# One more tile of layer-norm statistics ahead of the normalisation, in a fused attention and mixture layer on eight cores

## The chip, the cores and the metric

The kernel runs on the 8 cores of one Trainium2 chip. Cores 0 to 3 are one die, cores 4 to 7 the other. No core talks to another. The metric is device time in microseconds of the slowest core; a lower time is better.

## The reference

Input x is (4, 2048, 2048) float32. It is layer-normalised over its last axis, and the layer adds two branches to it:

```python
xn = layernorm(x)                        # no scale, no bias, eps 1e-5
q, k, v = xn @ Wq.T, xn @ Wk.T, xn @ Wv.T        # 16 heads of 128
attn = softmax(q k^T / sqrt(128)) v      # per head, over 2048 tokens
base = xn @ W_base.T + b_base
e = argmax(softmax(xn @ router_W.T))     # one of 8 experts
delta = ((xn @ A.T) * onehot(e)) @ Bw * 2.0      # rank 16 per expert
x = x + attn @ Wo.T + base + delta
```

## The kernel before

**Who does what.** Core c takes sequence c//2 and owns 1024 of its 2048 tokens. It computes keys and values for all 2048 tokens, and queries and outputs for its own. The host lays the tokens out so that a core's own come first (`xtok`).

**Stages.** First the layer-norm stage: 16 tiles of 128 tokens, each 128 x 2048 float32, 1 MB, are loaded, normalised to bf16, transposed on TensorE and left in `xnT` for good. Then `gen_proj` makes queries, keys and values of head 0, and for each head h attention of head h-1 is woven with the projections of head h. At the end come the output projection and the mixture branch (`gen_dpre`, `dpost`). Every matmul of a projection reads all of `xnT` (`XNALL`), so the first of them (L399) can start only when the last tile of the layer-norm stage is in `xnT`.

**The layer-norm stage.** Two functions write out its order by hand, each for one tile `tc`:

- `ln_stats(tc)` (L262 on): SyncE issues the load of the tile (L267) into one of four slots, `tc % 4`: slots 0 and 1 are the halves of `xst`, slots 2 and 3 lie in `pt`. VectorE runs four bn_stats of 512 columns (L271) and one bn_aggr (L275). ScalarE then makes 1/sqrt(var + eps) with Ln and Exp (L277, L280). `st2` and `rcol` have a place of their own for each tile.
- `ln_norm(tc)` (L284 on): VectorE writes (x - mean) * rstd as bf16 into one of two `xns` buffers (L290, one instruction of 2048 columns). TensorE transposes it in 16 pieces into two PSUM banks (L298), ScalarE copies the two banks into `xnT` (L302). Behind that stand the router's 16 small matmuls for tile `tc - 1` if that is below 8 (L329, copy L334), and, from `tc` 8 on, `mask_chain(tc - 8)`: two small VectorE instructions (L315, L317), a TensorE transpose (L320) and a ScalarE copy (L323).

**What sets the order.** Each engine runs its instructions in the order in which the program emits them. `Prog.emit` adds semaphore waits from the named reads and writes. A load of tile t writes the slot that tile t-4 had, so it waits in SyncE's queue until L290 of tile t-4, the last reader, is done. SyncE has only loads and stores to do, so it can run far ahead of the other engines otherwise. The emission loop is

```python
ln_stats(0)
ln_stats(1)
for tc in range(NTC):
    ln_norm(tc)
    ln_stats(tc + 2)
```

and gives VectorE the order S0 S1 N0 S2 N1 S3 N2 ... S15 N14 N15, where S is the statistics of a tile and N its normalisation (with the mask instructions behind N8 to N15). `ln_stats` returns at once for a tile past the last.

**The other loads.** GpSimd's queue issues, before any of this, the casting loads (float32 in HBM to bf16 in SBUF) of `ats`, `wbls` and head 0's `wqs`, `wks` and `wvs`, 1 MB of float32 each (L246 to L252, L378 to L386). They share the DMA engines with the tiles.

Of the kernel before, what the change touches and what calls it, by code (L numbers as in the profile page):

```python
# [147 lines left out]
def build_program(debug=False):  # L148
# [27 lines left out]
    with ExitStack() as st:  # L176
# [85 lines left out]
        def ln_stats(tc):  # L262
            if tc >= NTC:
                return
            sl = tc % 2
            xv, xk, ptk = xslots[tc % 4]
            p.emit("sync", lambda E, tc=tc, xv=xv: E.dma_start(  # L267
                xv, xtok[tc * 128:(tc + 1) * 128, :]), writes=[xk])
            s6 = st6[:, sl * 24:(sl + 1) * 24]
            for i in range(4):  # L270
                p.emit("dve", lambda E, xv=xv, i=i, s6=s6: E.bn_stats(  # L271
                    s6[:, i * 6:(i + 1) * 6], xv[:, i * 512:(i + 1) * 512]),
                    reads=[xk], writes=[f"st6{sl}"])
            s2 = st2[:, tc * 2:(tc + 1) * 2]
            p.emit("dve", lambda E, s6=s6, s2=s2: E.bn_aggr(s2, s6),  # L275
                   reads=[f"st6{sl}"], writes=[f"st2_{tc}"])
            p.emit("act", lambda E, s2=s2, sl=sl: E.activation(  # L277
                sqv[:, sl:sl + 1], s2[:, 1:2], AF.Ln, bias=epsc[:, 0:1],
                scale=1.0), reads=[f"st2_{tc}", "epsc"], writes=[f"sqv{sl}"])
            p.emit("act", lambda E, sl=sl, tc=tc: E.activation(  # L280
                rcol[:, tc:tc + 1], sqv[:, sl:sl + 1], AF.Exp, scale=-0.5),
                reads=[f"sqv{sl}"], writes=[f"rcol{tc}"])

        def ln_norm(tc):  # L284
            sl = tc % 2
            nxv, xk, ptk = xslots[tc % 4]
            xnv = xns[:, sl * D:(sl + 1) * D]
            xnk = f"xns{sl}"
            s2 = st2[:, tc * 2:(tc + 1) * 2]
            p.emit("dve", lambda E, nxv=nxv, xnv=xnv, s2=s2, tc=tc: E.tensor_scalar(  # L290
                xnv, nxv, s2[:, 0:1], rcol[:, tc:tc + 1],
                ALU.subtract, ALU.mult),
                reads=[xk, f"st2_{tc}", f"rcol{tc}"] + ptk, writes=[xnk])
            b0, b1 = (0, 1) if tc % 2 == 0 else (2, 3)
            for half, b in ((0, b0), (1, b1)):
                for j in range(8):
                    dc = half * 8 + j
                    p.emit("pe", lambda E, b=b, j=j, dc=dc, xnv=xnv: E.transpose(  # L298
                        psabf(b)[:, j * 128:(j + 1) * 128],
                        xnv[:, dc * 128:(dc + 1) * 128], idbf[:]),  # L300
                        reads=[xnk, "idbf"], writes=[f"psA{b}"])
                p.emit("act", lambda E, b=b, half=half, tc=tc: E.copy(  # L302
                    xnT3[:, half * 8:(half + 1) * 8, tc * 128:(tc + 1) * 128],
                    psabf(b).rearrange("p (a b) -> p a b", b=128)),
                    reads=[f"psA{b}"], writes=[f"xnT{tc}"])
            rtc = tc - 1
            if 0 <= rtc < 8:
                router(rtc)
            if tc >= 8:
                mask_chain(tc - 8)  # L310
# [26 lines left out]

        ln_stats(0)
        ln_stats(1)
        for tc in range(NTC):  # L340
            ln_norm(tc)
            ln_stats(tc + 2)

        def b2():
            for nb in range(2):
# [263 lines left out]
def _get_nc(debug=False):  # L609
    if debug not in _NC_CACHE:  # L610
        _NC_CACHE[debug] = build_program(debug)
    return _NC_CACHE[debug]
# [52 lines left out]
```

How the kernel before makes its waits and increments, by code:

```python
            def body(E, items=items, eng=eng):  # L133
                for it in items:
                    if it[0] == "w":
                        E.wait_ge(sem[it[1]], waitval(it[1], it[2]))
                    else:
                        instr = it[1](E)
                        sname = it[2]
                        if (sname, it[3]) in tgt:
                            instr.then_inc(
                                sem[sname],
                                16 if sname in self.dma_sems else 1)
```

## Time and profile before

| | us |
|---|---|
| median of 2 runs | 1332.82 (1332.25 to 1333.39) |
| the profiled execution, its time | 1330.53 |
| its span, slowest core (core 4) | 1329.0 |
| spans of the eight cores | 1323.3 to 1329.0 |
| first matmul of the first projection, core 4 | 98.97 |

The page and the answers below are of core 4 unless a line says otherwise. Times on a timeline count from the core's first instruction. PE is TensorE's matmuls, PEld its weight loads, DVE VectorE, ACT ScalarE, SPq SyncE's queue; "issue" is time in which an engine waited for nothing that the profile shows. On a timeline row the first number is the start, the second the duration (from the first start to the last end where instructions are merged), and the bracket is the engine's idle time before it with what ended it.

### The profile page before, as it was taken

The page shows a single profiled execution, that of the slowest core. Times are in us where ns is not written, and L with a number is a line of the kernel's source. Part 1 is how long each engine was busy: PE and PEld are TensorE (multiplying, and loading weights), DVE is VectorE, ACT ScalarE, POOL GpSimd, SP SyncE. Part 2 cuts the span into 40 slices and gives each one's busy share as a digit, 9 for nine tenths or more (in the row PEclk, how much of TensorE's full clock was granted, in tenths as well). Part 3 has the DMA queues.
Part 4 walks back from the last instruction along what each step waited for, and adds up shares of the span by engine and source line. Part 5 has one row for each costly group of instructions (what it writes and reads, how often), then busy time and mean ns, then how long its engine had stood idle before and what let it go on. Part 6 is the DMA issues. An engine that isn't in the chain of part 4 may idle for free.

```text
span 1329.0 us, 15178 instructions; the slowest of 8 cores (1323.3 to 1329.0 us)
## 1 busy us (share of the span) xinstructions
PE 1199.1 (90%) x5763; PEld 537.5 (40%) x5866; DVE 225.0 (17%) x326; ACT 403.1 (30%) x723; POOL 45.2 (3%) x89
## 2 busy tenths in 40 slices
PE   1449899999999999999999999999999997999998
PEld 1433444444443444444444434444444433444443
DVE  5871111111111111111111111111111100001001
ACT  2450233333343434333343433343333450000000
POOL 1000000000000000000000000000000000000000
PEclk9999999999999999999999999999999998999999
DMA  9831101112011111011010111110110304565774
GB/s 234 259 127 32 32 17 32 28 20 33 16 32 32 19 30 32 16 33 32 16 33 17 32 32 26 22 32 16 33 32 16 48 1 95 110 159 131 152 160 112
DMA packets 19255, 77.61 MB, mean 58 GB/s; under 512 B 2544, under 2 KB 2544, under 8 KB 17136
## 3 DMA queue, kind: packets, MB, share of 16 engines
q0 software_dynamic: 12128, 43.06, 20.2%
q1 hardware_dynamic: 7056, 33.57, 7.2%
q8 instruction: 49, 0.80, 0.2%
q14 instruction: 22, 0.18, 0.0%
HBM read 111.29 MB, written 8.39 MB: 90 GB/s over the span
## 4 chain that ended last, share of the span: by engine, by line
PE 85%; DVE 8%; DMA 4%; issue 3%; ACT 0%; DVEq 0%; SPq 0%; POOL 0%; ACTq 0%; POOLq 0%
PE psB L399 28%; PE psA L399 12%; PE psA L441 9%; PE psE L458 9%; PE psC L470 8%; PE psB L512 4%; PE psB L535 4%; PE psA L512 4%; PE psA L535 4%; DMA pt<-xtok 3%; DVE st L271 2%; DVE vt L409 2%; DVE kt L409 2%; DVE xns L290 1%; DMA wks<-wb 1%
## 5 line engine op out<-in xcount | busy, mean ns | idle before, releaser
L447 ACT ACTIVATE pt<-psA 128x512 bf16<-128x512 f32 x512 | 271.9, 600 | 353.8 <-PE psA L441 353.4
L399 PE MATMUL psB<-xnT,wvs 128*128 128x512 bf16 x751 | 216.1, 379 | 9.6 <-DVE kt L409 8.2
L399 PE MATMUL psA<-xnT,wks 128*128 128x512 bf16 x511 | 193.6, 379 | 9.0 <-DVE kt L409 8.2
L399 PE MATMUL psB<-xnT,wks 128*128 128x512 bf16 x496 | 185.3, 379 | 8.3 <-DVE qt L409 8.2
L441 PE MATMUL psA<-qt,kt 128*128 128x512 bf16 x510 | 143.0, 380 | 3.6 <-ACT vh L432 2.0
L399 PE MATMUL psB<-xnT,wqs 128*128 128x512 bf16 x497 | 118.7, 383 | 2.8 <-ACT maskT L323 2.0
L399 PEld LDWEIGHTS psB<-xnT,wvs 128*128 128x128 bf16 x768 | 74.0, 98 | 106.5 <-issue 21.6
L458 PE MATMUL psE<-pt,onesc 128*1 128x512 bf16 x512 | 115.7, 379 | 0.0
L470 PE MATMUL psC<-pt,vh 128*128 128x512 bf16 x482 | 109.4, 379 | 2.5 <-issue 2.5
L399 PE MATMUL psA<-xnT,wvs 128*128 128x512 bf16 x255 | 96.6, 379 | 0.1
L298 PE MATMUL psA<-idbf,xns 128*128 128x128 bf16 x256 | 29.9, 309 | 62.3 <-DVE xns L290 42.3
L480 DVE TENSOR_TENSOR ctall<-psC,bc 128x512 bf16<-128x512 f32 x32 | 22.1, 692 | 358.5 <-PE psA L441 311.8
L399 PEld LDWEIGHTS psB<-xnT,wks 128*128 128x128 bf16 x512 | 50.0, 98 | 72.3 <-issue 15.6
L399 PEld LDWEIGHTS psA<-xnT,wks 128*128 128x128 bf16 x512 | 50.0, 98 | 72.3 <-issue 15.6
L399 PEld LDWEIGHTS psB<-xnT,wqs 128*128 128x128 bf16 x512 | 50.5, 99 | 63.2 <-issue 4.2
L470 PEld LDWEIGHTS psC<-pt,vh 128*128 128x128 bf16 x512 | 47.5, 98 | 66.9 <-issue 14.0
L441 PEld LDWEIGHTS psA<-qt,kt 128*128 128x128 bf16 x512 | 47.5, 98 | 65.2 <-issue 13.9
L458 PEld LDWEIGHTS psE<-pt,onesc 128*1 128x1 bf16 x512 | 40.3, 83 | 67.5 <-issue 6.8
L512 PE MATMUL psB<-xnT,wks 128*128 128x512 bf16 x250 | 58.5, 387 | 6.1 <-DMA wks<-wb 5.7
L463 ACT ACTIVATE lnl<-psE 1x512 f32<-1x512 f32 x32 | 18.8, 586 | 136.7 <-PE psE L458 136.7
L535 PE MATMUL psB<-ctall,wqs 128*128 128x512 bf16 x252 | 58.0, 387 | 2.0 <-DVE ctall L480 1.8
L512 PE MATMUL psA<-xnT,vt 128*128 128x512 bf16 x251 | 57.1, 379 | 0.3
(68 smaller groups left out, 662.3 us busy)
## 6 DMA issues: line engine op xcount, KB each, us to landing
xst<-xtok SPq DMA_DIRECT2D x8, 1024.0 KB, 7.4
pt<-xtok SPq DMA_DIRECT2D x8, 1024.0 KB, 8.8
wqs<-wq POOLq DMA_DIRECT2D x16, 512.0 KB, 5.0
wks<-wk POOLq DMA_DIRECT2D x16, 512.0 KB, 5.2
wvs<-wv POOLq DMA_DIRECT2D x16, 512.0 KB, 5.0
xst<-xT SPq DMA_DIRECT2D x16, 512.0 KB, 12.0
outT<-outb SPq DMA_DIRECT2D x16, 512.0 KB, 11.1
wqs<-wo POOLq DMA_DIRECT2D x8, 512.0 KB, 8.3
```

What stands on the lines that cost most here:

```text
L271: p.emit("dve", lambda E, xv=xv, i=i, s6=s6: E.bn_stats(s6[:, i * 6:(i + 1) * 6], xv[:, i * 512:(i + 1) * 512]), reads=[xk], writes=[f"st6 ...
L298: p.emit("pe", lambda E, b=b, j=j, dc=dc, xnv=xnv: E.transpose(psabf(b)[:, j * 128:(j + 1) * 128], xnv[:, dc * 128:(dc + 1) * 128], idbf[: ...
L399: col=col, ws=ws: E.matmul(ps_t[:, col:col + 512], ws[:, dc * 128:(dc + 1) * 128], xnt(dc, nb * 512, (nb + 1) * 512), start=(dc == 0), sto ...
L409: dst=dst: E.tensor_copy(dst[:, nb * 512:(nb + 1) * 512], ps_t[:, col:col + 512]),
L441: p.emit("pe", lambda E, kc=kc, qb=qb, bk=bk, ktv=ktv, qtv=qtv: E.matmul(psa(bk), ktv[:, kc * 128:(kc + 1) * 128], qtv[:, qb * 512:(qb + 1 ...
L447: p.emit("act", lambda E, kc=kc, bk=bk: E.activation(pt[:, kc * 512:(kc + 1) * 512], psa(bk), AF.Exp, scale=SCALE), reads=[f"psA{bk}"], wr ...
L458: p.emit("pe", lambda E, kc=kc: E.matmul(psE[0:1, :], onesc[:], pt[:, kc * 512:(kc + 1) * 512], start=(kc == 0), stop=(kc == NTC - 1)), re ...
L463: p.emit("act", lambda E: E.activation(lnl[:], psE[0:1, :], AF.Ln), reads=["psE"], writes=["lnl"])
L470: p.emit("pe", lambda E, kc=kc, vhv=vhv: E.matmul(psC[:], vhv[:, kc * 128:(kc + 1) * 128], pt[:, kc * 512:(kc + 1) * 512], start=(kc == 0) ...
L480: p.emit("dve", lambda E, h=h, qb=qb: E.tensor_tensor(ctall[:, h * QOWN + qb * 512: h * QOWN + (qb + 1) * 512], psC[:], bc[:], ALU.mult), ...
L512: wbv=wbv, wbk_keys=wbk_keys, pk=pk: E.matmul(ps_t[:, off + nb * 512: off + (nb + 1) * 512], wbv[:, dc * 128:(dc + 1) * 128], xnt(dc, nb * ...
L535: p.emit("pe", lambda E, dc=dc, nb=nb, ps_t=ps_t, off=off, wot=wot: E.matmul(ps_t[:, off + nb * 512: off + (nb + 1) * 512], wot[:, dc * 12 ...
```

## The change

The loop gets one more call ahead of it, and its call inside runs three tiles ahead in place of two.

```diff
         ln_stats(0)
         ln_stats(1)
+        ln_stats(2)
         for tc in range(NTC):
             ln_norm(tc)
-            ln_stats(tc + 2)
+            ln_stats(tc + 3)
```

The buffers stay as they are: four slots for loaded tiles, two for normalised ones. No instruction is added or taken away. VectorE's order becomes S0 S1 S2 N0 S3 N1 S4 ... S15 N13 N14 N15; ScalarE's Ln and Exp of tile t stand behind the copies of tile t-3 in place of t-2. The order of the loads in SyncE's queue and what each waits for (L290 of tile t-4) are the same.

## Rows read from the trace of the kernel before

**Rows 1.** The page: header, busy time of the engines, 40 slices

```profile
span 1329.0 us, 15178 instructions; the slowest of 8 cores (1323.3 to 1329.0 us)
PE 1199.1 (90%) x5763; PEld 537.5 (40%) x5866; DVE 225.0 (17%) x326; ACT 403.1 (30%) x723; POOL 45.2 (3%) x89
PE   1449899999999999999999999999999997999998
DVE  5871111111111111111111111111111100001001
```

**Rows 2.** Timeline of TensorE, first round of the first projection; core 4, then core 7

```profile
98.97 8.47 PE L399 MATMUL psB<-xnT,wqs 128*128 128x512 bf16 x31 [2.02 <-ACT maskT L323]
...
99.72 7.07 PE L399 MATMUL psB<-xnT,wqs 128*128 128x512 bf16 x32 [1.64 <-ACT maskT L323]
```

**Rows 3.** Cores: span and mean granted TensorE clock

```profile
core 4: 1329.0 us, clock 0.996
...
core 7: 1328.3 us, clock 0.996
```

**Rows 4.** Waits of VectorE up to 98 us, longest first

```profile
DVE st L271 <- DMA xst<-xtok: 10.6, 4, 6.8
DVE st L271 <- DMA pt<-xtok: 4.8, 3, 1.8
```

**Rows 5.** Timeline of core 4, 18 to 44 us: statistics, normalisation, issues

```profile
18.48 3.08 DVE L271 BATCH_NORM_STATS2 st<-pt 128x6 f32<-128x512 f32 x4 [1.40 <-DMA pt<-xtok]
...
24.90 3.08 DVE L271 BATCH_NORM_STATS2 st<-pt 128x6 f32<-128x512 f32 x4 [1.78 <-DMA pt<-xtok]
...
28.27 1.34 DVE L290 TENSOR_SCALAR xns<-pt,st,rcol 128x2048 bf16<-128x2048 f32 x1
...
29.68 6.98 SPq L267 DMA_DIRECT2D pt<-xtok  x2
...
31.55 3.08 DVE L271 BATCH_NORM_STATS2 st<-xst 128x6 f32<-128x512 f32 x4 [1.94 <-DMA xst<-xtok]
...
43.68 3.09 DVE L271 BATCH_NORM_STATS2 st<-pt 128x6 f32<-128x512 f32 x4 [1.62 <-DMA pt<-xtok]
```

**Rows 6.** The same, 48 to 58 us

```profile
51.67 1.34 DVE L290 TENSOR_SCALAR xns<-pt,st,rcol 128x2048 bf16<-128x2048 f32 x1
...
52.92 3.08 DVE L271 BATCH_NORM_STATS2 st<-xst 128x6 f32<-128x512 f32 x4
53.08 4.95 SPq L267 DMA_DIRECT2D pt<-xtok  x2
...
57.54 3.08 DVE L271 BATCH_NORM_STATS2 st<-xst 128x6 f32<-128x512 f32 x4
```

**Rows 7.** DMA queues, 20 to 40 us: packets, MB, share of 16 engines

```profile
q0 software_dynamic: 458, 1.68, 52.0%
q1 hardware_dynamic: 458, 3.36, 51.0%
```

**Rows 8.** The same, from 71 us to the first projection

```profile
71.00 1.28 DVE L290 TENSOR_SCALAR xns<-pt,st,rcol 128x2048 bf16<-128x2048 f32 x1
72.66 3.08 DVE L271 BATCH_NORM_STATS2 st<-xst 128x6 f32<-128x512 f32 x4
...
88.08 3.08 DVE L271 BATCH_NORM_STATS2 st<-pt 128x6 f32<-128x512 f32 x4
91.44 1.28 DVE L290 TENSOR_SCALAR xns<-pt,st,rcol 128x2048 bf16<-128x2048 f32 x1
93.11 1.34 DVE L290 TENSOR_SCALAR xns<-pt,st,rcol 128x2048 bf16<-128x2048 f32 x1
93.97 2.17 ACT L302 COPY xnT<-psA 128x1024 bf16<-128x1024 bf16 x2 [1.76 <-PE psA L298]
96.19 2.15 ACT L302 COPY xnT<-psA 128x1024 bf16<-128x1024 bf16 x2
```

**Rows 9.** Loads issued from 48 to 83 us, median us to landing; core 4, then core 7

```profile
xst<-xtok SPq DMA_DIRECT2D x3, 1024.0 KB, 4.9
pt<-xtok SPq DMA_DIRECT2D x4, 1024.0 KB, 5.1
...
pt<-xtok SPq DMA_DIRECT2D x4, 1024.0 KB, 6.3
xst<-xtok SPq DMA_DIRECT2D x3, 1024.0 KB, 6.1
```

**Rows 10.** SyncE's timeline, the same tile's load on core 6, then core 7

```profile
53.62 0.33 SPq L267 DMA_DIRECT2D pt<-xtok  x1
...
54.21 0.33 SPq L267 DMA_DIRECT2D pt<-xtok  x1
```

## The prediction

> **What bounds the kernel now.** Read the page's busy shares and its 40 slices first [rows 1]. TensorE is busy 90% of the span, and from the fourth slice on (each is 33.2 us) it is full: there the time is set by matmuls, which this change does not touch. The first three slices are another stage: TensorE at 1, 4 and 4 tenths, VectorE at 5, 8 and 7. This is the layer-norm stage, and the first projection matmul, at 98.97 us on core 4 [rows 2], waits for its last copy. What moves that start moves the end by the same amount, since nothing behind it waits for a clock of its own. So the whole question is when L399 starts on each core. The spans of the cores [rows 3] say which core counts.
>
> Inside the stage, the waits of VectorE come next [rows 4]: it waited for seven loads, 15.4 us in all, of which 6.8 us is the first tile. The timeline tells two regimes apart. Up to 44 us VectorE idles 1.1 to 1.9 us before the statistics of each tile, until its load has landed [rows 5]. The tiles come every 6.3 us there (24.90 to 43.68 is three tiles). From 48 us on no load is waited for, and VectorE runs one tile in 4.62 us (52.92 to 57.54) [rows 6]; with the mask instructions, from tile 8 on, in 5.02. The first regime is bound by supply: the two DMA queues take 52% and 51% of the engines' time [rows 7], GpSimd's casting loads one half and the tiles the other. The second is bound by VectorE alone.
>
> **The change part by part.** No instruction is removed or added; VectorE's 96 large ones in this stage cost the same. Three things move.
>
> *First, the statistics wait less for their scale.* N(t) needs `rcol` from ScalarE. Before, one S stands between S(t) and N(t); after, two. But L290 shows no idle time before it [rows 5, 6, 8], only 0.18 us behind the aggregation, so nothing is won: zero.
>
> *Second, loads are issued one VectorE step later against their need.* A load of tile t is issued when N(t-4) is done. Before, VectorE had S(t-2), N(t-3), S(t-1) and N(t-2) to do from there to S(t), two periods; after, S(t-1) and N(t-3), one period. Four rows give the steps: statistics start to normalisation start 3.37 us (24.90 to 28.27), normalisation start to issue 1.4 (28.27 to 29.68), normalisation start to the next statistics 1.25 (51.67 to 52.92), or 1.66 with the mask instructions (71.00 to 72.66) [rows 5, 6, 8]. From issue to need that leaves 3.37 + 1.25 + 1.25 - 1.4 = 4.5 us in the plain tiles and 5.3 in those whose two normalisations carry masks. Before it was 4.6 to 5.0 us more, and landings of 4.9 to 6.3 us [rows 9] were hidden. Now they are not: of two tiles, one full chain is issue, landing, statistics, normalisation, so that two tiles cost L + 4.8 us and one costs (L + 4.8)/2, if that is over 4.62 (or 5.02). With core 4's landing, 4.9, this is 4.85; with core 7's, about 6.1, it is 5.45.
>
> I walked this through tile by tile for core 4. S2 starts at 18.48 and S3 at 24.90 as before, both set by landings. N0 moves behind S2, to 21.85, so tile 4 is issued at 23.2, where it was issued six microseconds earlier. It still queues behind tile 3, so that S4 comes at about 31.7 (31.55 before). How long before the landing of the tile ahead must a load be issued so that the queue does not run dry? The tiles' queue moved 3.36 MB, 3.2 tiles, in 51% of 20 us, which is 3.2 us of the engines for a tile [rows 7]; a tile that has them alone lands in 4.9 [rows 9]; the difference, 1.7 us, is what each load needs beside them (an estimate). Tiles 4, 5 and 6 are issued at 23.2, 29.7 and 36.6, and the tile ahead lands at 24.9, 31.7 and 37.9: 1.7, 2.0 and 1.3 us ahead, just enough or a little short. I allow 0.2 to 0.5 us for each: S5 at 37.9, S6 at about 44.7 against 43.68, or +1.0. (The empty time goes to the casting loads, which so end earlier.) Then S7 49.3, S8 54.4 (landing), S9 59.0, S10 63.9, S11 69.9 (the load of this tile took 6.1 us on core 4 before), S12 75.0, S13 80.4, S14 85.4, S15 90.65, against 88.08 [rows 8]. That is +2.6 us at S15. The bounds of this term: 0 if every landing shortens to what the gap hides, +2.6 with core 4's landings, +6.0 if I walk core 7 with its own (S15 at 95.25 against 89.21, with S6 0.7 late).
>
> *Third, the tail.* Behind S15 there were N14 and N15; now there are N13, N14 and N15. VectorE does a normalisation with its masks in 1.67 us (91.44 to 93.11), but ScalarE copies a tile in 2.22 (93.97 to 96.19) [rows 8], so the third tile costs ScalarE's time, not VectorE's. L399 started 7.53 us after N14 (98.97 - 91.44). Now it starts 7.53 + 2.21 = 9.74 us after N13, which is 3.37 after S15. From S15 to L399 it was 10.89 and becomes 13.1: +2.2 us. Were VectorE never late, S15 would come 1.67 earlier, having one normalisation less before it, and the tail would net +0.5; but S15 is held by loads from tile 3 on, so the whole 2.2 stands. Bounds +0.5 and +2.2; I take 2.2.
>
> The sum on core 4 is 2.6 + 2.2 = +4.8. On a core like 7 it is up to 6.0 + 2.2 = +8.2, and with L11's own slow landing and rounding in the walk, 8.7. I don't take the full value. Cores 0, 2, 5 and 7 show the long landings and 1, 3, 4 and 6 the short ones, and the long ones belong to the core of each pair that issues later: of cores 6 and 7 it is core 7, by 0.6 us [rows 10]. A core that falls behind its neighbour overlaps less with it, and its landing should approach 4.9. I take the middle between 4.8 and 8.7, +6.7.
>
> The Trainium skill, page "HBM Reference", section "Specifications (TRN2)", says that the two cores of a pair share one stack and get about 358 GB/s each when both stream. The page "DMA: Bandwidth & Descriptors" puts a fixed 2.0 us on each transfer. An estimate from the two is 1.05 MB/358 GB/s + 2.0 = 4.9 us for both cores. Core 4's row agrees, core 7's 6.1 to 6.3 does not; by the rule every core would lose 4.8.
>
> Which core ends last: core 4, 1329.0 + 4.8 = 1333.8; core 7, 1328.3 + 6.7 = 1335.0 [rows 3]. The slowest grows by 6.0 us, so the profiled execution's 1330.53 (1.5 us around its span) would become 1336.5. The median of the runs shown is 2.3 us above that execution, and the forecast against it is 1332.8 + 6.0 = 1338.8 us.
>
> **The rivals.**
>
> *The landings stay hidden or nearly so (chance 0.2).* Were the landings nowhere over 4.5 us, only the early 1.0 and the tail's 2.2 remain, +3.2; with an equal share in each pair and a clock gain (below) of 1.6 on core 4 it is 3.2 too. That gives 1333 to 1336. For it: the loads are later and farther apart, and casting loads end earlier. Against it: the medians behind 48 us are 4.9 and 5.1 even on core 4 [rows 9], and there the engines had little else to do.
>
> *Faster (chance 0.05).* One mechanism: TensorE's clock at the start of the projection. On core 4 the first round takes 8.4 us, on core 7 7.0 [rows 2]; 32 matmuls of 512 columns take 13.7 us at 1.2 GHz and 6.8 at 2.4, so core 4 began at the lower level and core 7 at the higher. Ahead of it both transposed two tiles close together. The granted clock in the records is 0.996 on both [rows 3] and doesn't tell them apart. With three tiles close together core 4 may enter at 2.4 GHz: -1.5 us on the slowest cores. It decides only if the loads cost nothing and the tail nets +0.5: 1332.8 - 1.0 = 1331.8. The first seven tiles' supply speaks against that.
>
> *Every late core pays in full (chance 0.2).* If the neighbour's traffic keeps landings at 6 us or over whatever the offset, core 7 loses 8.7: 1328.3 + 8.7 = 1337.0, +8.0, 1340.8. Should overlapping loads stretch to 7 us, the worst row among the late cores, each of the twelve tiles from 4 on costs (7 + 4.8)/2 - 5.0 = 0.9 more than before: 10.8 + 2.2 = 13, and 1345.
>
> *No change in what the program does (under 0.01):* the order of VectorE's queue must change, as emission order is queue order.
>
> **How the numbers follow.** My forecast, +4.8 to +8 us on the slowest core (1337 to 1341), has 0.55. Hidden landings have 0.2, the faster case 0.05, the full price 0.2. The time is that of the first, 1338.8. The range reaches down to the hidden case, 1333, and up to the stretched loads, 1345; about 0.1 stays out on each side. Two percent, which is about what a measurement of this kernel can tell from no change, is 26.7 us. No case comes near it, even the sum of the worst terms, 13: faster by over 2% 0.01, within 2% 0.98, slower by over 2% 0.01.
>
> **What would show it.** In the changed kernel VectorE's timeline must show waits for loads before the statistics of tiles 8 to 11 where there were none, and total waits for `xtok` of over 17 us on core 4 and over 20 on core 7. N0 starts near 21.9 us, the load of tile 4 is issued near 23.2, S15 starts near 90.7 on core 4, three normalisations stand 1.7 us apart behind it, and ScalarE's copies behind them 2.2 us apart; L399 starts near 103.8 on core 4 and near 106.4 on core 7. The prediction is wrong if landings fall under 4.5 us, if the supply in the first 45 us moves by more than 1 us per tile, or if what follows L399 is no longer the same length on each core.

## The result and the profile after

The changed kernel takes 1341.25 us (median) against 1333.25 us for the kernel before in the same comparisons. The ratio is 1.0058 with a 95% interval of 1.0045 to 1.0071: slower by 7.7 us or 0.6%, which is inside 2%. The forecast was 1338.8 us, the range 1333 to 1345. Some executions show one die disturbed; the ratios leave them out.

The answers of the profile of the changed kernel that correspond to [rows 3] (cores) come first, then VectorE's waits for loads on core 4, which [rows 4] show for before. A row of waits gives the total us, the count and the longest.

```profile
core 0: 1337.4 us, clock 0.995
...
core 4: 1329.3 us, clock 0.999
...
core 7: 1333.9 us, clock 0.995
```

```profile
DVE st L271 <- DMA xst<-xtok: 14.8, 5, 7.0
DVE st L271 <- DMA pt<-xtok: 6.5, 4, 2.3
```

The slowest core is now core 0. Core 4, the slowest before, hardly moved in this execution: 1329.3 against 1329.0. Spans alone would mislead here. The place to look is the start of the first projection round (the line is L400 now), on all eight cores:

| core | 0 | 1 | 2 | 3 | 4 | 5 | 6 | 7 | mean |
|---|---|---|---|---|---|---|---|---|---|
| start before, us | 99.92 | 98.81 | 99.52 | 98.75 | 98.97 | 99.27 | 99.14 | 99.72 | 99.3 |
| start after, us | 107.78 | 105.42 | 104.92 | 106.62 | 105.61 | 108.38 | 107.11 | 105.12 | 106.4 |
| later by | 7.9 | 6.6 | 5.4 | 7.9 | 6.6 | 9.1 | 8.0 | 5.4 | 7.1 |

So nearly the whole loss, 7.1 us on the mean, was made before that start, as the prediction said it must be; the spans are 7.4 us longer on the mean. What follows the first round takes the same time as before (1220.1 us against 1220.4, mean of the cores). The first round itself (32 matmuls, counted up to the first matmul of the next round) became 0.6 us longer on the mean, 8.0 against 7.5. Where part of it runs at TensorE's lower clock level (a matmul of 512 columns every 0.43 us and not every 0.22) it takes 8.1 to 8.7 us and not 6.7 to 6.9: before so on three cores, now on six. And the rest varies by core from 1217.0 us (core 4, granted clock 0.999) to 1222.7 (core 6, 0.996). Core 4 lost 6.6 us at the start, won 1.6 in the first round and 4.7 behind it.

Where in the stage did the loss arise? Below is VectorE's timeline on core 0 from 14 to 52 us, and from 95 us on with ScalarE's copies; it answers [rows 5] and [rows 8].

```profile
22.15 1.28 DVE L290 TENSOR_SCALAR xns<-xst,st,rcol 128x2048 bf16<-128x2048 f32 x1
25.45 3.09 DVE L271 BATCH_NORM_STATS2 st<-pt 128x6 f32<-128x512 f32 x4 [2.02 <-DMA pt<-xtok]
...
35.27 3.09 DVE L271 BATCH_NORM_STATS2 st<-xst 128x6 f32<-128x512 f32 x4 [5.17 <-DMA xst<-xtok]
...
41.18 3.08 DVE L271 BATCH_NORM_STATS2 st<-xst 128x6 f32<-128x512 f32 x4 [1.20 <-DMA xst<-xtok]
```

```profile
95.06 3.08 DVE L271 BATCH_NORM_STATS2 st<-pt 128x6 f32<-128x512 f32 x4
...
98.42 1.28 DVE L290 TENSOR_SCALAR xns<-xst,st,rcol 128x2048 bf16<-128x2048 f32 x1
...
100.08 1.34 DVE L290 TENSOR_SCALAR xns<-pt,st,rcol 128x2048 bf16<-128x2048 f32 x1
100.95 2.17 ACT L302 COPY xnT<-psA 128x1024 bf16<-128x1024 bf16 x2 [1.76 <-PE psA L298]
...
102.16 1.34 DVE L290 TENSOR_SCALAR xns<-pt,st,rcol 128x2048 bf16<-128x2048 f32 x1
...
103.17 2.15 ACT L302 COPY xnT<-psA 128x1024 bf16<-128x1024 bf16 x2
...
105.38 2.15 ACT L302 COPY xnT<-psA 128x1024 bf16<-128x1024 bf16 x2
```

The reader sees two of the three costs. Tile 4 is waited for, 5.17 us, where [rows 5] show 1.94 on core 4. At the end three copies stand 2.2 us apart, where there were two. The third cost lies between. It is read from the starts of the statistics, as means over the eight cores:

| statistics of tile | 3 | 4 | 5 | 6 | 7 | 9 | 11 | 13 | 15 | first projection |
|---|---|---|---|---|---|---|---|---|---|---|
| before, us | 25.1 | 31.9 | 37.8 | 44.3 | 48.9 | 58.1 | 68.2 | 78.6 | 88.7 | 99.3 |
| after, us | 25.1 | 35.5 | 41.3 | 46.1 | 52.5 | 62.4 | 73.1 | 83.2 | 93.6 | 106.4 |
| later by | 0 | 3.6 | 3.4 | 1.8 | 3.6 | 4.2 | 4.8 | 4.6 | 4.9 | 7.1 |

Tile 4 loses 3.6 us, half of it comes back by tile 6, tile 7 loses it again, and tiles 9 and 11 add 0.6 us each. VectorE waits for the load of these two on every core (0.2 to 1.4 us), never for that of tile 8 and at most 0.14 us for that of tile 10: its load is issued before the wait for tile 9, and lands in that time. From tile 15 to the projection it is 12.8 us, before 10.6.

Why is tile 4 so late? Its load was issued at 23.51 us on core 0, and tile 3 landed near 25. The DMA queues from 24 to 26 us (packets, MB, share of 16 engines; q1 holds the tiles, q0 GpSimd's casting loads), first in the kernel before, then in the changed one, and the time from issue to landing of tile 4 in the changed one:

```profile
q1 hardware_dynamic: 53, 0.38, 54.3%
q0 software_dynamic: 54, 0.17, 52.4%
```

```profile
q0 software_dynamic: 101, 0.35, 107.9%
q1 hardware_dynamic: 8, 0.00, 0.6%
```

```profile
xst<-xtok SPq DMA_DIRECT2D x1, 1024.0 KB, 11.7
```

The tiles' queue moves next to nothing for two microseconds, though a load of 1 MB was issued half a microsecond before they began. The casting loads take the engines whole. The queue's share is 35% from 27 to 28 us and 58% from 28 to 30, so the bytes of tile 4 began to flow about 4 us after its issue. The load of tile 5 was issued at 30.2 us, 5 us ahead of the landing of tile 4, and followed on: q1 holds 49% to 59% from 35 to 38 us. This text calls it a dry queue when a load is issued so shortly before the landing of the one ahead that the queue's share falls to nothing in between. Why the bytes then take 4 us to start is not shown. In return the casting loads end sooner: the last of them, `wvs`, landed 36.1 us after its issue instead of 40.9 on core 0. From there on the tiles have the engines alone, and that is where tile 6 wins back 1.7 us.

### The profile page after: what moved, and what is told of

Same layout as the page of the kernel before. It is cut to its first block, busy times and chain, and to the rows that moved or that the text cites. A ratio compares the mean times of both kernels' runs of the same rounds, so it can differ in the third digit from the quotient of the medians.

```text
span 1337.4 us, 15282 instructions; the slowest of 8 cores (1329.3 to 1337.4 us)
## 1 busy us (share of the span) xinstructions
PE 1207.8 (90%) x5866; PEld 537.3 (40%) x5866; DVE 225.4 (17%) x326; ACT 403.0 (30%) x723; POOL 45.4 (3%) x89
## 4 chain that ended last, share of the span: by engine, by line
PE 85%; DVE 7%; DMA 5%; issue 2%; ACT 0%; DVEq 0%; SPq 0%; POOL 0%; ACTq 0%; POOLq 0%
PE psB L400 28%; PE psA L400 12%; PE psA L442 9%; PE psC L471 9%; PE psE L459 8%; PE psB L513 4%; PE psB L536 4%; PE psA L513 4%; PE psA L536 4%; DMA pt<-xtok 3%; DVE st L271 2%; DVE vt L410 2%; DVE kt L410 2%; DMA xst<-xtok 1%; DVE xns L290 1%
## 5 line engine op out<-in xcount | busy, mean ns | idle before, releaser
L400 PE MATMUL psB<-xnT,wvs 128*128 128x512 bf16 x768 | 217.5, 379 | 8.7 <-DVE kt L410 8.2
L400 PE MATMUL psA<-xnT,wks 128*128 128x512 bf16 x512 | 193.9, 379 | 8.2 <-DVE kt L410 8.2
L400 PE MATMUL psB<-xnT,wks 128*128 128x512 bf16 x512 | 191.3, 379 | 8.2 <-DVE qt L410 8.2
L400 PE MATMUL psB<-xnT,wqs 128*128 128x512 bf16 x512 | 119.7, 383 | 1.8 <-ACT maskT L323 1.8
L400 PEld LDWEIGHTS psB<-xnT,wvs 128*128 128x128 bf16 x768 | 74.0, 98 | 106.5 <-issue 21.5
L471 PE MATMUL psC<-pt,vh 128*128 128x512 bf16 x512 | 116.0, 380 | 0.0
L400 PE MATMUL psA<-xnT,wvs 128*128 128x512 bf16 x256 | 97.0, 379 | 0.0
L400 PEld LDWEIGHTS psB<-xnT,wks 128*128 128x128 bf16 x512 | 49.9, 98 | 72.4 <-issue 15.6
L400 PEld LDWEIGHTS psA<-xnT,wks 128*128 128x128 bf16 x512 | 49.9, 98 | 72.3 <-issue 15.6
L400 PEld LDWEIGHTS psB<-xnT,wqs 128*128 128x128 bf16 x512 | 50.5, 99 | 63.3 <-issue 4.1
L513 PE MATMUL psB<-xnT,wks 128*128 128x512 bf16 x256 | 59.3, 388 | 5.3 <-DMA wks<-wb 5.3
## 6 DMA issues: line engine op xcount, KB each, us to landing
xst<-xT SPq DMA_DIRECT2D x16, 512.0 KB, 10.6
```

What stands on the lines that cost most here:

```text
L400: col=col, ws=ws: E.matmul(ps_t[:, col:col + 512], ws[:, dc * 128:(dc + 1) * 128], xnt(dc, nb * 512, (nb + 1) * 512), start=(dc == 0), sto ...
L471: p.emit("pe", lambda E, kc=kc, vhv=vhv: E.matmul(psC[:], vhv[:, kc * 128:(kc + 1) * 128], pt[:, kc * 512:(kc + 1) * 512], start=(kc == 0) ...
L513: wbv=wbv, wbk_keys=wbk_keys, pk=pk: E.matmul(ps_t[:, off + nb * 512: off + (nb + 1) * 512], wbv[:, dc * 128:(dc + 1) * 128], xnt(dc, nb * ...
```

## The experiments

All times "at the start" below are those of the first projection matmul, as means over the eight cores of the profiled execution: 99.3 us in the kernel before, 106.4 in the changed one. Single cores of one kernel lie 1 to 4 us apart, and 6 in after_late_casts, so that differences of these means under about 0.5 us say little. A timeline row that ends with its window counts only the instructions inside it, so `x1` or `x2` at L271 or L272 are the first of a tile's four. In the cuts below `...` stands for lines left out; where the slot of a tile changes, the line in `ln_norm` that picks it changes in the same way.

**A fifth slot (after_5slots).** It gives the loads back the distance that they had, and leaves the changed order.

```diff
-                  (ptf[:, D:2 * D], "xs3", [...])]
+                  (ptf[:, D:2 * D], "xs3", [...]),
+                  (outb[:], "xs4", ["outb0", "outb1"])]
...
-            xv, xk, ptk = xslots[tc % 4]
+            xv, xk, ptk = xslots[tc % 5]
```

> The changed order (statistics three tiles ahead), with a fifth slot for loaded tiles, which lies in the output buffer, unused in this stage. A load of tile t then waits for the normalisation of tile t-5 and has two periods of VectorE again until it is needed. Theory (loads are exposed): tile 4 is queued from the start, its statistics begin near 31.5 us instead of 35 to 36.7, no wait for a load stands behind 48 us, and what is left of the loss is the tail, 2.2 us: the first projection matmul 2.0 to 2.5 us later than in the kernel before on each core (101 to 102.5), against 5.4 to 9.1 us later in the changed kernel. Time about 1335 to 1336. Rival (the loss is in the order of the engines' work, loads are a by-product): it stays at +5 us or more.

Ratio 1.0016 (1.0006 to 1.0026); start at 100.6, +1.3 us. Tile 4's statistics on core 0, then VectorE's waits there from 47 us to 100:

```profile
31.06 1.49 DVE L272 BATCH_NORM_STATS2 st<-outb 128x6 f32<-128x512 f32 x2 [1.43 <-DMA outb<-xtok]
```

```profile
DVE mask L318 <- DVE mxc L316: 0.9, 5, 0.2
DVE mask L318 <- PE psC L321: 0.8, 2, 0.5
DVE st L272 <- DVE st L272: 0.5, 1, 0.5
```

No load is left among the waits of this core. On cores 1, 2 and 4 tile 7 still waits 0.8 to 1.1 us (until 49.20 on core 4), so "none behind 48 us" was not met everywhere. The start is less late than I expected, 1.3 and not 2.0 to 2.5, because the last statistics come 0.9 us earlier than before (87.8 against 88.7). Of the 7.1 us, 5.8 go with the fifth slot: the loads make the loss, the order a small part.

**Three slots with the order of before (before_3slots).** The reverse: only the loads lose distance.

```diff
-            xv, xk, ptk = xslots[tc % 4]
+            xv, xk, ptk = xslots[tc % 3]
```

> The order of the kernel before (two tiles ahead), with three slots for loaded tiles in place of four. The order of VectorE's work, and so the tail, stay as before; only the loads lose one period, as in the changed kernel. Theory: the waits of the changed kernel come back, one tile earlier: the tiles' queue runs dry behind tile 2, the statistics of tile 3 wait 4 us or more, and the first projection matmul comes 3.5 to 6 us later than before (102.5 to 106), with 10.5 to 10.9 us from the last statistics to it. Rival (the tail and the order make the loss): within 1 us of before.

Ratio 1.0038 (1.0025 to 1.0051); start at 102.9, +3.6. The dry queue is back, one tile earlier. Statistics of tile 3 on core 0, and the queues from 19 to 22 us:

```profile
29.45 0.69 DVE L271 BATCH_NORM_STATS2 st<-xst 128x6 f32<-128x512 f32 x1 [6.33 <-DMA xst<-xtok]
```

```profile
q0 software_dynamic: 126, 0.46, 96.4%
q1 hardware_dynamic: 5, 0.04, 4.3%
```

So with no change of order at all, a shorter distance from issue to need slows the kernel, by the waits and at the places that the changed kernel shows.

**The tail alone (late_switch).** Two tiles ahead up to tile 13, three from there on.

```diff
-            ln_stats(tc + 2)
+            if tc < 11:
+                ln_stats(tc + 2)
+            if tc == 11:
+                ln_stats(13)
+            if tc >= 11:
+                ln_stats(tc + 3)
```

> Two tiles ahead up to tile 13, then three: VectorE's order ends S13 S14 N12 S15 N13 N14 N15 as in the changed kernel, but the loads of tiles 4 to 13 keep the distance they had before. Theory: the last statistics come 1.7 us earlier, having one normalisation less in front, and the path from them to the first projection matmul is 2.0 to 2.2 us longer: net +0.3 to +0.6 us at that matmul, no wait for a load behind 48 us. Rival (three normalisations in a row cost 2.2 us wherever they stand): +2.2 us. As for TensorE's clock: if three tiles' transposes close together brought it to its upper level, the first round would take 7.0 us on all cores; in the changed kernel it took 8.2 to 8.7 on six of eight.

Ratio 1.0009 (0.9997 to 1.0021); start at 99.1, -0.2 us: no loss that can be told. (This execution was 0.7 us ahead of the kernel before at the statistics of tile 13, where the two orders are still the same; set against that, the order costs 0.5 us, within the 0.3 to 0.6 expected.) The end of core 0's stage shows how the two halves cancel. The last statistics start at 86.66 and not at 89.41, three normalisations follow, and the projection starts 12.7 us later, where it was 10.5:

```profile
86.66 3.08 DVE L271 BATCH_NORM_STATS2 st<-pt 128x6 f32<-128x512 f32 x4
90.02 1.28 DVE L290 TENSOR_SCALAR xns<-xst,st,rcol 128x2048 bf16<-128x2048 f32 x1
91.68 1.34 DVE L290 TENSOR_SCALAR xns<-pt,st,rcol 128x2048 bf16<-128x2048 f32 x1
93.75 1.34 DVE L290 TENSOR_SCALAR xns<-pt,st,rcol 128x2048 bf16<-128x2048 f32 x1
```

Its first round takes 8.1 to 9.6 us on all eight cores. But that does not mean that the transposes left TensorE at its lower level. Below is core 0 of the changed kernel, whose first round starts at 107.78 us and takes 8.6: a row gives the stretch, its length, busy time and number of instructions of PE, PEld, DVE, ACT and POOL, then the granted clock, the share of the DMA engines and GB/s.

```profile
104.70:108.00 3.30, 1.03 (x13) 0.63 (x12) 0.00 (x0) 2.83 (x5) 0.00 (x0) 1.00 0.00 0
108.10:111.40 3.30, 3.30 (x10) 1.15 (x8) 0.00 (x0) 0.00 (x0) 0.00 (x0) 0.50 0.00 0
111.50:116.30 4.80, 4.80 (x24) 2.16 (x22) 0.00 (x0) 0.00 (x0) 0.00 (x0) 1.00 0.00 0
```

The full clock, 2.4 GHz, is granted from 104.7 us, while the third tile is transposed. Then TensorE idles 1.84 us, and from 108.1 to 111.5 us the clock is half, 1.2 GHz. In the seven kernels that end with three normalisations the full clock is granted 1.9 to 5.1 us ahead of the first round on all 56 cores, and on 49 of them it is halved again for a stretch that reaches into the round. In the four that end with two it is granted ahead of the round on 14 of 32 cores, and halved again on 2; on the other 18 the round begins with a matmul about every 0.4 us, and the record of the clock starts, at full, 2.8 to 5.9 us into it.

**Casting loads behind tile 10 (after_late_casts).** The changed order, four slots. The five issues at the start, of `ats`, `wbls` and head 0's weights, are taken out.

```diff
+        def late_casts():
+            gate = ["st2_10"]
+            p.emit("pool", lambda E: E.dma_start(
+                wqs[:], ...), reads=gate, writes=["wqs"])
+            # then wks, wvs, ats, wbls
...
             ln_stats(tc + 3)
+            if tc + 3 == 10:
+                late_casts()
```

> The changed order with four slots; the five casting loads of 1 MB are issued only once the statistics of tile 10 are done, so nothing shares the DMA engines with the tiles before. Theory (the tile queue dried up while the casting loads had the engines): the load of tile 4, issued near 20 us, lands in about 4.9 us and not in 11.6; the waits of 5 to 6 us before tile 4 go, VectorE waits 0.2 to 1 us per tile for landings, the last statistics start at 80 to 84 us and the first projection matmul at 93 to 97, 3 to 6 us earlier than in the kernel before. Rival (the delay of tile 4 is a fixed cost of a load issued late, whatever else runs): tile 4 still takes 8 us or more.

Half right. Ratio 1.0075 (1.0053 to 1.0097); start at 106.8, where I expected 93 to 97. Landing of tile 4 and then of tile 13 on core 0, and the queues from 64 to 80 us:

```profile
xst<-xtok SPq DMA_DIRECT2D x1, 1024.0 KB, 4.8
```

```profile
xst<-xtok SPq DMA_DIRECT2D x1, 1024.0 KB, 12.6
```

```profile
q0 software_dynamic: 431, 1.57, 59.3%
q1 hardware_dynamic: 303, 2.22, 42.4%
```

Tile 4, issued at 20.6 us on this core, landed in 4.8 us, not in 11.7: the delay is no fixed cost of a late load. Up to tile 11 the stage ran 10.5 us ahead of the changed kernel (62.6 against 73.1). But the loads of tiles 12 to 15 are issued from 60 us on, beside the casting loads and with the short distance. Those of tiles 12 to 14 took 9 to 13.5 us, that of tile 15 6 to 8.5, and the whole gain was lost again. I had overlooked that four loads were still to be issued.

**A slot for tile 4 alone (after_tile4_slot).** The changed kernel, tile 4 in the output buffer.

```diff
-            xv, xk, ptk = xslots[tc % 4]
+            xv, xk, ptk = xslots[4 if tc == 4 else tc % 4]
```

> The changed kernel; only tile 4 has a slot of its own (in the output buffer), so its load is queued from the start and tile 8, the next in slot 0, waits for no one either. All other loads keep the short distance. It parts the two costs of the loads: the dry tile queue at 24 to 27 us, and the landings that show later. Theory: statistics of tile 4 at 31 to 32 us in place of 35 to 36.7; tiles 5, 6, 7 still wait for loads, as do 9 to 11 a little; the first projection matmul comes 3.5 to 5.5 us later than before, where the changed kernel is 5.4 to 9.1 later. If the dry queue were the whole cost of the loads, it would be 1.3 us as with five slots; if it cost nothing, since the casting loads get done earlier, it would be as late as the changed kernel.

A miss. Ratio 1.0054 (1.0039 to 1.0069); start at 105.8, +6.6 where I expected 3.5 to 5.5. Tiles 4 and 5 on core 0, and its queues from 30 to 33 us:

```profile
30.20 3.08 DVE L272 BATCH_NORM_STATS2 st<-outb 128x6 f32<-128x512 f32 x4 [1.39 <-DMA outb<-xtok]
...
40.50 1.49 DVE L272 BATCH_NORM_STATS2 st<-xst 128x6 f32<-128x512 f32 x2 [5.60 <-DMA xst<-xtok]
```

```profile
q0 software_dynamic: 137, 0.50, 100.4%
q1 hardware_dynamic: 4, 0.03, 3.0%
```

Tile 4 is in time, and the queue runs dry before tile 5 instead. The distance is the matter, not one tile.

**Everything early: eight slots, casting loads behind tile 10, both orders (before_late_casts_8slots and after_late_casts_8slots).**

```diff
+        ctf = ctall[:].bitcast(F32)
+        xslots += [(ctf[:, i * D:(i + 1) * D], f"xs{4 + i}", ["ct"])
+                   for i in range(4)]
...
-            xv, xk, ptk = xslots[tc % 4]
+            xv, xk, ptk = xslots[tc % 8]
```

> The order of the kernel before, with eight slots for loaded tiles (four more in the attention output buffer, unused in this stage), and the five casting loads issued only once the statistics of tile 10 are done; by then the load of every tile has been issued. Theory: nothing but VectorE bounds the stage. Tiles land 3.2 us apart, VectorE takes 4.62 us for one and 5.02 with the mask instructions: statistics of tile 2 begin near 16 us, of tile 15 at 79 to 80, the first projection matmul at 89.5 to 91, 9 us earlier than in the kernel before; no wait for a load behind 15 us. Time about 1323. Rival: the casting loads, now together at 57 to 75 us, are late for the first projection, or slow ScalarE and VectorE, and the gain is under 5 us.

> The same with the changed order (three tiles ahead). With every load early, what is left between this kernel and the last one is the order alone: the last statistics come 1.7 to 2.1 us earlier (one normalisation less in front of them, and its mask instructions), the path from there to the first projection matmul is 2.2 us longer, so that matmul comes 0.1 to 0.6 us later than in the kernel with the order of before. Rival (the changed order has a cost of its own beyond the loads): 2 us or more later.

With the order of before: ratio 0.9929 (0.9903 to 0.9955), start at 90.4. With the changed order: 0.9938 (0.9920 to 0.9957), start at 91.2. The difference, 0.8 us in the profiled executions, is what the order costs when loads cost nothing: the last statistics come 1.4 us earlier (78.4 against 79.8) and the way from there is 2.2 us longer. That is a little over the 0.1 to 0.6 expected. The two ratios overlap, so that the times alone don't show it.

**Casting loads behind the last tile's load, four slots, both orders (before_last_casts, gate on tile 13; after_last_casts, gate on tile 14).** The edit is that of the late casting loads with another gate. Its change of place also puts head 0's weights ahead of `ats` and `wbls` in GpSimd's queue, in all five kernels that have it.

> The kernel before with its four slots; the five casting loads are issued once the statistics of tile 13 are done, which is after the last tile's load was issued. Theory: with nothing beside the tiles, four slots and two periods of distance hide every landing: as with eight slots, the first projection matmul at 90 to 91 us and no wait for a load behind 15 us; time 1323 to 1325. Rival: four slots are too few even so, or the casting loads now come too late for the first projection: a gain under 5 us.

> The same with the changed order and four slots, the casting loads behind the statistics of tile 14. No queue shares the DMA engines with any tile, so no dry queue can cost more than the landing itself: what is left of the loss against the run before is the exposed landings and the order (0.8 us). Theory: loads land in 4.7 to 6.4 us, VectorE waits 0.2 to 2 us before some of the tiles 4 to 11, 4 to 6 us in all; the first projection matmul comes 4 to 6 us after that of the last kernel (94.5 to 96.5). If the dry queue beside casting loads were the whole cost of the loads, it would be 1 us after it; if the landings alone made all of the 7.1 us, 7.

With the order of before: ratio 0.9936 (0.9920 to 0.9951), median 1322.85 us, start at 90.5. With the changed order: 0.9995 (0.9978 to 1.0012), 1329.74 us, start at 95.5, that is 5.1 us later. VectorE's waits on core 0 from 19 us on, with the order of before (the first row is the wait for the first projection round) and then with the changed one:

```profile
DVE qt L422 <- PE psB L412: 10.3, 1, 10.3
DVE mask L314 <- DVE mxc L312: 1.4, 6, 0.5
DVE mask L314 <- PE psC L317: 0.5, 1, 0.5
```

```profile
DVE st L268 <- DMA pt<-xtok: 2.4, 3, 1.1
DVE st L268 <- DMA xst<-xtok: 2.4, 2, 1.5
```

This pair isolates the second cost. Nothing else is loaded beside the tiles from 19 us on, and still five loads show, 4.8 us on this core, since loads of 4.8 to 6.0 us do not fit into the 4.5 us from issue to need.

**The account.** 5.1 us are landings and order together (last pair); the order is 0.8 of them (the pair with eight slots), the landings 4.3. The rest of the 7.1, 2.0 us, is there only beside casting loads, and I put it down to the dry queue, less what the earlier end of the casting loads gives back; no run holds it alone. This assumes that the parts add. The fifth slot gives 5.8 for all loads and 1.3 for the rest, which agrees within the scatter.

The version that beats both kernels is the order of before with the casting loads issued last: 0.6% faster than before with four slots (0.9936) and 0.7% with eight (0.9929), which can't be told apart. The simpler one needs no new buffer.

## Why the prediction was right, and where it was not

**Right: where and why.** Behind the first projection matmul only the first round changed length on the mean, by 0.6 us. The scale was waited for in neither kernel. The distance from issue to need fell from two periods to one, and VectorE now waits before tiles that had no wait: for loads 21.3 us in all on core 4 and 21.0 on core 7, where over 17 and over 20 were forecast. The tail came out as worked out: 2.2 us more on the mean of the cores, 2.0 on core 4 (92.68 to 105.61, against 88.08 to 98.97). Both halves of that step show in late_switch, which nets about nothing. The kernel is slower by 7.7 us, and the slowest core was forecast to lose 6.0.

**Two of the prediction's three signs of being wrong came.** The supply in the first 45 us moved by more than 1 us per tile: tile 4 by 3.6 and tile 5 by 3.4. And what follows the start of the projection is not the same length on each core: it became 6.4 us shorter on core 4 and 5.5 longer on core 6. The mean moved by 0.2 only, so this is scatter between cores and no cost of the change. The third, landings under 4.5 us, did not: the shortest from tile 4 on took 4.6. Of the waits foreseen before tiles 8 to 11 only those before 9 and 11 came on all cores.

**Mis-sized: the early part.** The prediction allowed 0.2 to 0.5 us per tile for a queue that runs dry, and put tile 6 at +1.0. The step that failed is its estimate of 1.7 us between issue and the flow of bytes, taken as landing time less transfer from loads that had the engines to themselves. Beside a full casting queue tile 4's bytes flowed about 4 us after its issue. So tile 4 lost 3.6 us, not 0.2. My note that the empty time goes to the casting loads was right, and explains why half of it came back by tile 6, on the mean +1.8.

**Mis-sized: what the early part hands on.** For core 4 the walk had +2.6 us at the statistics of tile 15; core 4 shows 92.68 against 88.08, +4.6, and the mean is +4.9. The later landings are not what it lacked: from tile 7 to tile 15 the walk had 41.35 us, and core 4 shows 40.6 (39.8 before). All that is missing stands at tile 7. The walk had it at 49.3, +1.0; it began at 52.05 on core 4, +3.7, waiting 1.3 us for a load issued late because tiles 4 and 5 had been. A delay in the supply stretch is handed on through the slots: tile 7's load waits for the normalisation of tile 3, which waits for the statistics of tile 5.

**Wrong: which cores pay.** The prediction gave the long landings to the core of each pair that issues later, and took that to be cores 0, 2, 5 and 7 again, with up to +8.7 on core 7 and +4.8 on core 4. Core 7 lost 5.4 and core 4 6.6. The rule held, but the cores changed. In the changed kernel the later ones at tile 8 are 0, 3, 5 and 6, and they lost 7.9, 7.9, 9.1 and 8.0; their partners lost 5.4 to 6.6. In before_last_casts the later cores are 1, 3, 5 and 6, with median landings of 5.4 to 6.0 us from tile 4 on, against 4.7 to 4.9 on the others. On three pairs most of the difference is there at tile 7 (+4.5 to +5.0 us against +2.1 to +3.7), on cores 0 and 1 it arises behind it. Behind 50 us the medians of the changed kernel lie at 4.7 to 5.3 on all cores, first core 5, then core 7:

```profile
xst<-xtok SPq DMA_DIRECT2D x4, 1024.0 KB, 5.2
```

```profile
xst<-xtok SPq DMA_DIRECT2D x4, 1024.0 KB, 4.9
```

From tile 11 on partners issue 1.8 to 3.0 us apart, where it was 0.5 to 1.1 before, and the split between them nearly closed, as the prediction thought it might. The 4.9 us for both cores that it had estimated from the Trainium skill ("HBM Reference", "Specifications (TRN2)", and the fixed cost in "DMA: Bandwidth & Descriptors", "Anatomy of one DMA") is close to what these rows show. That the total of 6.0 us was near the mark is luck in part: the early part was put too small, the later landings on cores 4 and 7 too large, and the wrong choice of the late cores does not show in the time of the slowest.

**The rivals.** Hidden landings: refuted by the waits. Faster by TensorE's clock: refuted in its result, not in its first half. Three tiles' transposes close together did bring the full clock ahead of the first round on all 56 cores, but it did not last: the round was slow (7.9 us or more) on 49 of 56 cores, and with two at the end, counting before, on 20 of 32. Every late core pays in full (its upper case, 1332.8 + 13, makes 1345.8 and not 1345): this is the size that came (+8.0 by the medians, and 7.9 to 9.1 on the four late cores), but landings did not stay at 6 us or over, so not by that mechanism.

## What to carry to other kernels

Calling a stage further ahead does not load further ahead: with the number of buffers fixed, every step by which the consumer's last read is put off is taken from the distance between a load's issue and its need. Count that distance in periods before and after, and compare it with the landing time. Where another queue keeps the DMA engines full, a queue that runs empty costs more than the landing time of a lone load suggests; the first remedy is to issue what is not needed yet behind the last urgent load, but truly behind it.

## What the runs showed of the hardware

With both queues filled, each had about half of the engines' time (52% and 51% in [rows 7]). When the tiles' queue had run dry, the casting queue took 108% of a 2 us window by the records, and a tile's load issued 0.5 us before that window put 0.6% of q1 into it. The same load, issued with no casting load about, landed in 4.8 us and not in 11.7.

The loads of tiles 7 and 11 took longer than most of their neighbours, whatever time they were issued at: 5.6 to 7.1 and 5.6 to 6.4 us in the changed kernel (near 46 and 67 us), 5.5 to 6.3 and 5.5 to 6.2 in after_last_casts (near 36 and 56), where 4.8 is common. It is not the tile. With three slots the long one is tile 10 (5.3 to 6.0 us) and tile 11 is not; with five it is tile 12 (5.5 to 7.3). What these loads share is a packet of 16 KB of another DMA queue (q8, which the profile calls instruction) on the engines while they are under way: in the changed kernel and in both kernels with the casting loads last it falls into the loads of tiles 7 and 11, and into no other from tile 4 on, on all eight cores; with three slots it falls into tile 10 too, with five into tile 12, on all eight. Not every long load has one (with three slots tile 14 took 5.3 to 5.6 us without it). Part of tile 7's wait in the changed kernel goes with it. That the packet is the cause is not shown: no run moved it alone.

The first projection round ran either in 6.7 to 6.9 us or in 7.9 to 9.8, core by core. In the slow ones 6 to 14 matmuls come about every 0.43 us, and in the kernels with three normalisations at the end the granted clock is recorded at 0.50 there. The full clock that the transposes had brought was kept on 7 of 56 cores and lost on 49, in the changed kernel after a stretch in which TensorE did the end of the last transposes and then idled 1.8 to 2.1 us. But core 4 idled 1.95 us there and kept it. What decides was not settled; no run was made for it alone.
